# Two interleaved transformer layers on one core: a slot between producer and consumer at the seams, and layer norm's centring folded into the expert weights

## The chip, the cores and the metric

One core of one Trainium2 chip runs the whole model. The time is the device time of the core in microseconds (us), and the median of the runs counts. The core has TensorE (PE in the profile, its weight loads PEld), VectorE (DVE), ScalarE (ACT), GpSimd (POOL) and SyncE (SP, which issues all DMAs). Every engine works through its own stream of instructions in order, and semaphores tie the streams together.

## The reference, cut to what matters

The input is 4 sequences of 1024 tokens with 128 features. Four blocks follow one another, each with a residual and a layer norm:

```
x = layernorm(x + mamba(x))          # conv of 4 taps, 256 channels x 16 states, scan over time
x = layernorm(x + moe16(x))          # 16 experts of 64, top 2, and a shared one of 352, SiLU
x = layernorm(x + lstm_attention(x)) # LSTM of 20 cells over time, gives place and width of a Gaussian
x = layernorm(x + 4 x moe4(x))       # 4 layers of 4 experts of 512, top 2, GELU
```

Each of the four layers of the last block (layer 1's FFN) computes

```
logits = x @ router_w + rb;  comb = top-2 softmax weights
xhat = (x - mean(x)) * rsqrt(var(x) + 1e-5)
y_e = gelu((xhat * g_e + b_e) @ w1_e + b1_e) @ w2_e + b2_e
x = sum_e comb_e * (x + y_e)
```

All of it is in float32.

## The kernel before, in words

Time is cut into 8 chunks of 128 tokens (512 columns over the 4 sequences). The LSTM needs 1024 steps one after another; a step goes PE (gates, L905), ACT (L915, L916), DVE (L929, L932, L935), ACT (L919), DVE (L940). All other work is laid between these steps by hand. `period(i)` lays out 128 **slots**. In slot t each engine's stream gets the LSTM step t of chunk i, and then, in this order, one piece (up to a generator's next `yield`) of `layer1(i-1)`, `layer0(i+1)`, and of the Mamba work for chunk i+2 (`scan`, `leave`) and i+3 (`pre`, `soft`). A piece is what stands between two `yield`s, and the same piece number falls in the same slot on all engines. So where producer and consumer are in the same piece number, the consumer's engine waits inside the slot; where they are one piece apart, the result is usually there already.

- `layer1` of chunk q: attention for `att_slots(q)` = 18+q slots, then 4 layers of `LAYER` = 23 slots, then a last norm of 5 slots. In a layer, slots o = 0 to 4 are the norm and the router, o = 5 to 22 the experts (v = 0 to 17): the first product of unit v, L656, GELU, L714, the second product of unit v-2, L666.
- The norm (`norm_pe`, `norm_act`, `norm_dve`, `norm_pool`, L338 to L389): the mean by a product with a matrix of 1/128 (L337, in the layers two products, L623 and L625), centring (L372), square (L362), variance (L347), +EPS (L376), power -0.5 on POOL (L388), its rows by a product (L354), scaling (L381).
- The router (`choose_dve`, L395 to L428), the transposed weights `combT` (L644, L706), the load of the GELU table (L707) and of the exp table (L717, after the last GELU, o = 20).
- `layer0`: the 16-expert FFN in 11 units, each of three pieces: gate product (L465), up product (L469), down product (L475) on PE, tanh (L515) on ACT, three products by element on DVE (L556, L561, L546). It runs in the slots that are not `heavy` (o = 6 to 21 are heavy), from slot 4 on.
- `scan`: 64 pieces for 32 states, one in each heavy slot (L1197, L1206 on DVE, L1135, L1139, L1154 on POOL). `burst`: the decays (L1226, ACT), 8 per layer, in slots o = 22, 0, 1, 2, 3, behind all else in the slot.
- `pre`: conv of chunk i+3 (taps L955, SiLU L1007 and L1011, L983, L988, L995), after the last layer's slots.
- Period 0 has no layer 1; `fold` runs there: for each of the 16 experts of the four layers, b @ w1 (L1284) and w1 times g (L1299), stored to DRAM.
- Before period 0 the opening does chunks 0 and 1 of Mamba (`unit`) and layer 0 of chunk 0; period 8 has only layer 1 of chunk 7, without the LSTM.

The order in a slot, from `period`:

```
next(lstm, None)
if layer1: next(layer1, None)
heavy = layer1 is not None and slot >= att and 6 <= o < LAYER - 1 and slot < tail
if layer0 and not (heavy and slot < CH) and slot >= (L0_AT if layer1 else 0):
    next(layer0, None)
...
    elif heavy: advance(scan, "scan", SCAN)
    if layer1 and att - 1 <= slot < tail - 2:
        for _ in range({22: 1, 0: 2, 1: 2, 2: 2, 3: 1}.get(o, 0)): next(burst, None)
```

## Time and profile before

| | |
|---|---|
| median of 3 runs | 3133.24 us (3132.89 to 3133.72) |
| profiled execution, its own time | 3143.73 us |
| its span, first to last instruction | 3141.7 us |
| busy: PE / DVE / ACT / POOL | 81% / 62% / 44% / 34% of the span |
| granted TensorE clock, mean | 0.803 of 2.4 GHz |

The rows further down are of the profiled execution. No engine is busy all the time; the LSTM step ties them together, and a slot lasts as long as its slowest way round.

### The profile page before, as it was taken

What the parts mean: (1) busy time and instruction counts of PE and PEld (TensorE: products, weight loads), DVE (VectorE), ACT (ScalarE), POOL (GpSimd) and SP (SyncE); (2) the same over time, 40 slices, a digit from 0 to 9 for tenths busy, and PEclk for the clock granted to TensorE, in tenths of its full rate; (3) what the DMA queues carried; (4) which work ended last, traced back from release to release, by engine and by line L of the source; (5) the groups of instructions that cost most, each with busy time, mean ns of one, the idle gap of its engine ahead of it and who ended that gap; (6) DMA issues with size and microseconds to landing.
All of it is one profiled execution on the core that took longest, in us unless ns stands there. A gap on an engine that the chain in (4) does not pass through costs nothing.

```text
span 3141.7 us, 30770 instructions
## 1 busy us (share of the span) xinstructions
PE 2537.0 (81%) x7208; PEld 1271.2 (40%) x7208; DVE 1943.4 (62%) x6569; ACT 1386.7 (44%) x4620; POOL 1062.8 (34%) x913
## 2 busy tenths in 40 slices
PE   4776884479996989789886998788978997889598
PEld 1122443244444444344444443444444444444344
DVE  4857587357775777567766677577766555444422
ACT  3232433435544555445544554445534444444233
POOL 4735257104542445235432455244422001100200
PEclk7587655659996899878996899789978996788699
DMA  3231332003321233113220332122311220111021
GB/s 108 68 84 54 89 99 72 25 13 100 101 66 28 80 96 90 42 46 101 78 71 27 92 97 75 25 73 84 92 33 46 65 64 21 34 64 58 10 81 57
DMA packets 111774, 204.70 MB, mean 65 GB/s; under 512 B 14799, under 2 KB 24422, under 8 KB 111592
## 3 DMA queue, kind: packets, MB, share of 16 engines
q1 hardware_dynamic: 111592, 202.75, 22.1%
q8 instruction: 57, 0.93, 0.1%
q14 instruction: 125, 1.02, 0.1%
HBM read 195.36 MB, written 7.34 MB: 65 GB/s over the span
## 4 chain that ended last, share of the span: by engine, by line
PE 41%; DVE 28%; ACT 14%; issue 7%; POOL 1%; DVEq 0%; POOLq 0%; ACTq 0%
PE p_hid L656 8%; DVE state L1197 7%; PE p_turn L905 7%; PE p_misc L666 4%; ACT cell_t L919 4%; DVE cell L935 3%; DVE add_c L932 3%; PE p_acc L666 3%; DVE weighed L1206 2%; DVE p_turn L929 2%; PE p_misc L354 2%; PE p_gate L465 2%; DVE hist L940 2%; PE p_turn L475 1%; ACT cand L916 1%
## 5 line engine op out<-in xcount | busy, mean ns | idle before, releaser
L905 PEld LDWEIGHTS p_turn<-hist,w_hh 22*128 22x128 f32 x2048 | 371.6, 225 | 1148.2 <-DVE hist L940 1013.9
L905 PE MATMUL p_turn<-hist,w_hh 22*128 22x4 f32 x2048 | 457.3, 291 | 420.2 <-DVE hist L940 402.2
L656 PE MATMUL p_hid<-xhat,w 128*128 128x512 f32 x1024 | 581.8, 652 | 1.1 <-ACT hid L714 0.7
L919 ACT ACTIVATE cell_t<-cell 20x4 f32<-20x4 f32 x1024 | 207.7, 203 | 701.7 <-DVE cell L935 701.7
L1135 POOL TENSOR_TENSOR drive<-du,rows 128x512 f32<-128x512 f32 x256 | 473.4, 1849 | 63.2 <-DVE state L1197 44.9
L929 DVE SCALAR_TENSOR_TENSOR p_turn<-p_turn,cell 20x4 f32<-20x4 f32 x1024 | 170.7, 167 | 500.8 <-ACT p_turn L915 478.9
L714 ACT ACTIVATE hid<-p_hid,b1f 128x512 f32<-128x512 f32 x512 | 351.6, 687 | 243.1 <-PE p_misc L666 151.1
L388 POOL TENSOR_TENSOR n_rstd<-n_var,minus_half 128x4 f32<-128x4 f32 x56 | 62.0, 1108 | 1098.3 <-DVE n_var L376 1098.3
L1197 DVE TENSOR_TENSOR_SCAN state<-decay,drive 128x512 f32<-128x512 f32 x256 | 398.1, 1555 | 25.2 <-POOL drive L1139 15.7
L1154 POOL TENSOR_TENSOR y<-y,weighed 128x512 f32<-128x512 f32 x192 | 242.4, 1262 | 450.5 <-DVE weighed L1206 449.9
L940 DVE SCALAR_TENSOR_TENSOR hist<-p_turn,cell_t 20x4 f32<-20x4 f32 x1024 | 162.7, 159 | 275.6 <-ACT cell_t L919 275.6
L915 ACT ACTIVATE p_turn<-p_turn 96x4 f32<-96x4 f32 x1024 | 157.8, 154 | 349.1 <-PE p_turn L905 345.7
L666 PE MATMUL p_acc<-hid,w 128*128 128x512 f32 x512 | 275.3, 621 | 0.0
L666 PE MATMUL p_misc<-hid,w 128*128 128x512 f32 x512 | 264.1, 598 | 0.0
L1206 DVE TENSOR_TENSOR weighed<-state,rows 128x512 f32<-128x512 f32 x256 | 184.7, 722 | 7.9 <-DVE state L1197 0.5
L916 ACT ACTIVATE cand<-p_turn 32x4 f32<-32x4 f32 x1024 | 171.9, 168 | 25.2
L935 DVE SCALAR_TENSOR_TENSOR cell<-p_turn,add_c 20x4 f32<-20x4 f32 x1024 | 157.9, 154 | 35.3
L656 PEld LDWEIGHTS p_hid<-xhat,w 128*128 128x128 f32 x1024 | 160.3, 191 | 42.5 <-issue 26.5
L1169 PE MATMUL p_hid<-weighed,ident 128*128 128x512 f32 x128 | 113.7, 986 | 78.9 <-DVE weighed L1206 78.9
L1226 ACT ACTIVATE decay<-delta,a_neg 128x508 f32<-128x508 f32 x256 | 174.6, 710 | 2.2
L932 DVE SCALAR_TENSOR_TENSOR add_c<-p_turn,cand 20x4 f32<-20x4 f32 x1024 | 154.8, 151 | 31.6
L1139 POOL TENSOR_TENSOR drive<-drive,kc 128x4 f32<-128x4 f32 x256 | 143.2, 559 | 20.1
(204 smaller groups left out, 3161.5 us busy)
## 6 DMA issues: line engine op xcount, KB each, us to landing
rows<-rows_dram SPq DMA_DIRECT2D x128, 512.0 KB, 5.0
w<-w_dram SPq DMA_DIRECT2D x128, 256.0 KB, 2.7
w<-in_w2T SPq DMA_DIRECT2D x128, 256.0 KB, 2.7
comb_b<-comb_dram SPq DMA_DIRECT2D x64, 512.0 KB, 4.7
rows<-comb_dram SPq DMA_DIRECT2D x128, 128.0 KB, 2.9
w<-in_w1T SPq DMA_DIRECT2D x16, 256.0 KB, 2.8
w_dram<-w SPq DMA_DIRECT2D x16, 256.0 KB, 2.4
out_xT<-result SPq DMA_DIRECT2D x8, 256.0 KB, 2.5
```

Of the source, the lines that this page charges most:

```text
L656: nc.tensor.matmul(p_hid[:, v % 2, :], w1[:, v // FB, (v % FB) * P:(v % FB + 1) * P], xhat[:, :], start=True, stop=True).then_inc(g_h, 1)
L666: nc.tensor.matmul((p_misc1, p_acc1)[e % 2][:, :], w2[:, e, f, :], hid1[:, w % 2, :], start=(f == 0), stop=(f == FB - 1)).then_inc(g_y, 1)
L714: nc.scalar.activation(hid1[:, v % 2, :], p_hid[:, v % 2, :], ACT.Gelu, bias=b1f[:, l * UN + v:l * UN + v + 1]).then_inc(g_gelu, 1)
L905: nc.tensor.matmul(gate_bank(i)[:, :, t:t + 1], w_hh[:, :], before, start=False, stop=False, skip_group_check=True).then_inc(gates_done, 1)
L919: nc.scalar.activation(cell_t[64:64 + PE_, :], cell[32:32 + PE_, :], ACT.Tanh, scale=0.5).then_inc(cell_tanh, 1)
L929: nc.vector.scalar_tensor_tensor(out=gate(32), in0=gate(32), scalar=1.0, in1=cell[32:32 + PE_, :], op0=ALU.add, op1=ALU.mult).then_inc(kee ...
L932: nc.vector.scalar_tensor_tensor(out=add_c[32:32 + PE_, :], in0=gate(0), scalar=1.0, in1=cand[0:PE_, :], op0=ALU.add, op1=ALU.mult).then_i ...
L935: nc.vector.scalar_tensor_tensor(out=cell[32:32 + PE_, :], in0=gate(32), scalar=0.5, in1=add_c[32:32 + PE_, :], op0=ALU.mult, op1=ALU.add) ...
L1135: nc.gpsimd.tensor_tensor(flat(drive[:, n % 2, :, :]), du[:, j, :], rows[:, (u * S + s_) % ROWS, 0, :], ALU.mult).then_inc(driven, 1)
L1154: nc.gpsimd.tensor_tensor(y[:, j, :], y[:, j, :], weighed[:, n % 2, :], ALU.add).then_inc(y_summed, 1)
L1197: nc.vector.tensor_tensor_scan(flat(state[:, n % 2, :, :]), flat(decay[:, n % RING, :, :]), flat(drive[:, n % 2, :, :]), 0.0, ALU.mult, AL ...
L1206: nc.vector.tensor_tensor(weighed[:, n % 2, :], flat(state[:, n % 2, :, :]), rows[:, (u * S + s_) % ROWS, 1, :], ALU.mult).then_inc(weighe ...
```

## The change

- **Norm of the four expert layers.** The mean of w1 over its rows is taken off each expert's w1 once (in `fold`), so that `xhat` needs no centring: the square is taken of x itself, the mean comes as a fifth column of the router's product, and the variance is E[x2] + EPS - mean2. The two mean products (L623, L625) and the centring (L372) go for l = 0 to 3; the norm behind the last layer keeps them. New small DVE instructions: a copy of the mean, its square, and a subtraction in the place of the +EPS.
- **Norm slots.** Square in slot 0, variance products in 1, tanh in 2, `comb` in 3, rstd rows and xhat in 4. `combT`'s products move from slot 4 to v = 0, into another bank, its copy on ACT to v = 1 (o = 6), and its DMAs follow one slot later. The exp table is loaded one slot later (v = 16).
- **Fold.** Per expert one product of 128x512 more on PE and one subtraction of 128x512 on DVE, in the same piece.
- **Layer 0.** ACT's tanh and the DVE pieces behind it come one piece later; the down sum, the last norm and the copy get pieces between them (55 pieces for 52). It starts in slot 1 and leaves out slot o = 22.
- **Attention.** The third row product comes second, one DVE instruction of 128x512 less, the scans in two halves; one slot more (`att_slots` 19+q).
- **Conv (`pre`).** The second pair of taps comes a piece earlier, the SiLU of the second block, the second z product and its SiLU a piece later; one piece fewer in all.
- **Scan in the opening.** The product that sums `weighed` k on PE comes in the piece after the one that makes it.
- **Decays** come before layer 1 and layer 0 in ACT's stream.

```diff
@@ layer1_pe, per layer
-            ln = norm_pe(n1, q * NL + l, src, (n1.src_ready, q * NL + l + 1), logits, (lambda: mean_of_two(n)) if l else None)
-            for s_ in range(5):
-                next(ln)
-                if s_ == 4:
-                    pe.wait_ge(g_comb, n + 1)
-                    for j in range(B):
-                        mm = nc.tensor.transpose(p_hid[0:E1, 1, j * P:(j + 1) * P], comb1[:, j, :], ident[:, :])
-                    mm.then_inc(g_combT, 1)
+            pe.wait_ge(n1.src_ready, q * NL + l + 1)
+            for j in range(B):
+                mm = nc.tensor.matmul(p_hid[:, 0, j * (E1 + 1):(j + 1) * (E1 + 1)], tile(src, j), w_router1[:, l, :],
+                                      start=True, stop=True)
+            mm.then_inc(g_logit, 1)
+            yield
+            pe.wait_ge(n1.square_done, q * NL + l + 1)
...
+            for _ in range(3):
                 yield
+            pe.wait_ge(n1.rstd_done, q * NL + l + 1)
...
+                if v == 0:
+                    pe.wait_ge(g_comb, n + 1)
+                    for j in range(B):
+                        mm = nc.tensor.transpose(tile(p_acc1, j)[0:E1, :], comb1[:, j, :], ident[:, :])
+                    mm.then_inc(g_combT, 1)
@@ layer1_act, per layer
+            act.wait_ge(n1.src_ready, q * NL + l + 1)
+            if l:
+                act.wait_ge(n1.var_done, q * NL + l)
+            nc.scalar.activation(n1.square[:, :], src, ACT.Square).then_inc(n1.square_done, 1)
+            yield
+            yield
+            choose_act(n, arg1, tanh1, g_arg, g_tanh)
+            yield
+            yield
+            act.preload_act_table(ACT.Gelu)
+            yield
...
-                    if v == UN - 1 and l < L - 1 and q + 3 < NCH:
-                        act.preload_act_table(ACT.Exp)
+                if v == 1:
+                    act.wait_ge(g_combT, n + 1)
+                    if n:
+                        act.wait_ge(g_comb_stored, 16 * n)
+                    nc.scalar.copy(combT1[:, :], p_acc1[0:E1, :]).then_inc(g_combT_taken, 1)
+                if v == UN and l < L - 1 and q + 3 < NCH:
+                    act.preload_act_table(ACT.Exp)
@@ layer1_dve, per layer
+            yield
+            next(ch)
+            nc.vector.tensor_copy(mean1[:, :], p_hid[:, 0, 0:B * (E1 + 1)].rearrange("p (b e) -> p b e", b=B)[:, :, E1:E1 + 1]
+                                  .rearrange("p b o -> p (b o)")).then_inc(mean_step, 1)
+            next(ch)
+            dve.wait_ge(mean_step, 2 * n + 1)
+            nc.vector.tensor_tensor(mean1[:, :], mean1[:, :], mean1[:, :], ALU.mult).then_inc(mean_step, 1)
+            yield
+            dve.wait_ge(mean_step, 2 * n + 2)
+            dve.wait_ge(n1.var_done, q * NL + l + 1)
+            nc.vector.scalar_tensor_tensor(out=n1.var[:, :], in0=p_acc1[:, 448:448 + B], scalar=EPS, in1=mean1[:, :],
+                                           op0=ALU.add, op1=ALU.subtract).then_inc(n1.var_taken, 1)
+            next(ch)
+            yield
+            next(ch, None)
+            yield
+            dve.wait_ge(n1.rstd_rows, q * NL + l + 1)
+            nc.vector.tensor_tensor(xhat[:, :], src, p_misc1[:, :], ALU.mult).then_inc(n1.out_done, 1)
+            yield
@@ mamba_scan_pe
+            if early and k:
+                sum_y(k - 1)
             yield
-            if early:
-                pe.wait_ge(weighed_done, n + 1)
-                nc.tensor.matmul(p_hid[:, j, :], ident[:, :], weighed[:, n % 2, :], start=False, stop=(k >= NS - NB),
-                                 skip_group_check=True).then_inc(y_summed, 1)
             yield
@@ fold_pe
+            pe.wait_ge(fold_grown, k + 1)
+            if k:
+                pe.wait_ge(fold_scaled, k)
+            nc.tensor.matmul(p_misc1[:, :], mean_w[:, :], w1[:, k % E1, :], start=True, stop=True).then_inc(fold_mean, 1)
@@ fold_dve
+            yield
+            dve.wait_ge(fold_mean, k + 1)
+            nc.vector.tensor_tensor(w1[:, k % E1, :], w1[:, k % E1, :], p_misc1[:, :], ALU.subtract).then_inc(fold_scaled, 1)
@@ period
-    L0_AT = 4
+    L0_AT = 1
+    BURST = {LAYER - 1: 1, 0: 1, 1: 2, 2: 2, 3: 2}
...
+            if u < NCH and layer1 and att - 1 <= slot < tail - 2:
+                for _ in range(BURST.get(o, 0)):
+                    next(burst, None)
             if layer1:
                 next(layer1, None)
-            if layer0 and not (heavy and slot < CH) and slot >= (L0_AT if layer1 else 0):
+            last = layer1 is not None and att < slot < tail and o == LAYER - 1
+            if layer0 and not ((heavy or last) and slot < CH) and slot >= (L0_AT if layer1 else 0):
```

## Rows read from the trace of the kernel before

**Rows 1.** The page's head, and the granted TensorE clock in 40 slices:

```profile
span 3141.7 us, 30770 instructions
...
PEclk7587655659996899878996899789978996788699
```

**Rows 2.** Timeline of one bare LSTM step, period 2, slot 122 (start, us, what [idle before]):

```profile
1308.53 0.59 PE L905 MATMUL p_turn<-hist,w_hh 22*128 22x4 f32 x2 [1.57 <-DVE hist L940]
1309.15 0.15 ACT L915 ACTIVATE p_turn<-p_turn 96x4 f32<-96x4 f32 x1 [0.87 <-PE p_turn L905]
...
1309.33 0.17 DVE L929 SCALAR_TENSOR_TENSOR p_turn<-p_turn,cell 20x4 f32<-20x4 f32 x1 [0.86 <-ACT p_turn L915]
...
1310.12 1.28 ACT L1062 ACT_TABLE_LOAD   x1
1310.14 0.16 DVE L940 SCALAR_TENSOR_TENSOR hist<-p_turn,cell_t 20x4 f32<-20x4 f32 x1 [0.27 <-ACT cell_t L919]
```

**Rows 3.** Sums by stretch: the opening, period 0, period 3 (columns in the first row):

```profile
core 0: us, PE busy (x) PEld busy (x) DVE busy (x) ACT busy (x) POOL busy (x), PEclk, DMA share, GB/s
0.00:330.63 330.63, 210.69 (x352) 72.52 (x352) 212.57 (x228) 94.93 (x197) 171.91 (x161) 0.71 0.28 77
330.63:646.18 315.55, 193.68 (x536) 122.85 (x536) 202.03 (x671) 120.14 (x488) 132.19 (x114) 0.54 0.23 69
...
1319.42:1659.08 339.66, 293.22 (x856) 144.02 (x856) 234.35 (x816) 170.66 (x575) 138.92 (x117) 0.86 0.24 71
```

**Rows 4.** Seams of seven slots: worst, best, sums of 20 (periods 1-5), period 6, period 7:

```profile
1433.64:1458.88 25.24, 23.30 (x65) 11.64 (x63) 13.89 (x62) 13.18 (x37) 2.81 (x4) 0.71 0.21 59
...
2066.49:2085.04 18.55, 15.13 (x61) 7.91 (x60) 12.51 (x60) 14.21 (x39) 2.94 (x3) 1.00 0.19 60
...
sum 431.55, PE 387.38 PEld 199.26 DVE 271.06 ACT 270.22 POOL 57.73; mean PE 19.37 PEld 9.96 DVE 13.55 ACT 13.51 POOL 2.89
...
sum 75.08, PE 67.62 PEld 33.70 DVE 54.58 ACT 33.14 POOL 4.53; mean PE 16.91 PEld 8.43 DVE 13.65 ACT 8.29 POOL 1.13
...
sum 69.64, PE 55.27 PEld 37.73 DVE 36.01 ACT 28.77 POOL 4.03; mean PE 13.82 PEld 9.43 DVE 9.00 ACT 7.19 POOL 1.01
```

**Rows 5.** The same 20 stretches, the mean products of L623 and of L625 alone:

```profile
sum 431.55, PE 20.34 PEld 5.27; mean PE 1.02 PEld 0.26
...
sum 431.55, PE 15.35 PEld 6.32; mean PE 0.77 PEld 0.32
```

**Rows 6.** Single slots of period 3: o = 22, o = 1, and o = 19, 20 (columns as in rows 3):

```profile
1498.12:1501.99 3.87, 3.87 (x13) 1.54 (x12) 2.67 (x8) 1.90 (x6) 0.35 (x1) 0.85 0.42 157
...
1505.03:1507.90 2.87, 2.40 (x12) 1.48 (x12) 2.36 (x18) 2.38 (x7) 0.00 (x0) 1.00 0.00 0
...
1425.62:1428.00 2.38, 2.29 (x6) 0.97 (x6) 1.98 (x7) 1.11 (x4) 1.18 (x3) 1.00 0.64 195
1428.00:1431.32 3.32, 1.44 (x4) 0.59 (x4) 2.02 (x6) 2.59 (x6) 2.69 (x3) 0.95 0.19 72
```

**Rows 7.** Timeline of the worst seam's slot o = 0 (6.36 us long):

```profile
1439.05 0.69 DVE L372 TENSOR_TENSOR mdrive<-xl,p_misc 128x512 f32<-128x512 f32 x1 [1.68 <-PE p_misc L625]
...
1440.73 0.60 ACT L515 ACTIVATE silu<-p_gate 128x512 f32<-128x512 f32 x1 [3.55 <-PE p_gate L465]
...
1441.36 1.33 ACT L1226 ACTIVATE decay<-delta,a_neg 128x508 f32<-128x508 f32 x2
```

**Rows 8.** Who waited for whom over the whole run (us, times, longest):

```profile
PE p_hid L1169 <- DVE weighed L1206: 78.9, 60, 16.3
...
ACT xd L1007 <- PE p_hid L955: 28.5, 7, 8.6
...
ACT xd L1011 <- PE p_hid L955: 17.7, 8, 2.7
```

**Rows 9.** Period 0, 14 slots with fold and layer 0: stretch, and its costliest PE group:

```profile
383.40:427.63 44.23, 39.28 (x97) 21.27 (x96) 38.41 (x88) 14.99 (x61) 23.92 (x22) 0.57 0.43 134
...
L465 PE MATMUL p_gate<-mid_x,w_gate 128*128 128x512 f32 x10 | 9.4, 1042 | 0.0
```

**Rows 10.** The opening beside layer 0, 15 of chunk 1's 32 scans (columns as in rows 3):

```profile
191.50:251.10 59.60, 43.57 (x89) 16.06 (x87) 51.53 (x61) 19.23 (x45) 26.74 (x30) 0.97 0.35 96
```

**Rows 11.** Period 8, from the last expert's sum to the next layer's first product:

```profile
3016.44:3025.21 8.77, 6.70 (x33) 4.56 (x31) 4.90 (x26) 0.84 (x2) 1.01 (x1) 0.80 0.17 60
```

201 lines of the change are left out of this document (107 added, 94 removed).

## The prediction

> **What bounds the kernel now.** I read the page first, then one bare LSTM step, then sums by stretch, by seam and by slot, then the waits. The page has no full engine, and a granted TensorE clock that moves between tenths 5 and 9 [rows 1]. The bare step shows what a slot costs at least. From one L940 to the next it takes 1.83 us, and in it ACT is idle 0.87 us before L915 and DVE 0.86 us before L929 [rows 2]. So what else a slot gives to ACT or DVE is free up to about 0.9 us and then lengthens the slot one for one; PE has some 1.2 us (1.57 us idle, less its own turn-round). A period has 128 slots, 234 us if all were bare; period 3 takes 339.66 [rows 3]. The excess is in three places. The heavy slots (2.38 us for a plain one [rows 6]) hardly change. The **seams**, the seven slots o = 22, 0 to 5 between two expert layers, take 431.55 us for the 20 of periods 1 to 5, 21.58 each, and 18.8 and 17.4 in periods 6 and 7 [rows 4]. The rest is attention, the conv behind the last layer, and period 0.
>
> In a seam PE is busy 19.37 of 21.58 us, but 15.13 of 18.55 where the clock was 1.00, and 23.30 of 25.24 where it was 0.71 [rows 4]. So a seam has about 15.1 us of PE work at 2.4 GHz, and what makes the bad ones is that work at half clock with consumers waiting in the same slot. The worst slot says it: centring waited 1.68 us for the mean, layer 0's tanh 3.55 us for its gate product, and two decays of 1.33 us stood behind the tanh, ahead of the next LSTM step [rows 7].
>
> **The parts, costed.** The sum is made against the profiled execution, 3143.7 us, 10.5 above the median of the runs; I take the difference off the median.
>
> *Seams of periods 1 to 5.* The two mean products go: 1.02 + 0.77 = 1.79 us of PE a seam [rows 5], and with them the centring, 0.69 us of DVE [rows 7]. Slot 22 loses layer 0's piece. Slot by slot, with a 512-column ACT or DVE instruction at 0.6 to 0.75 us:
> - o = 22: DVE has 0.75 + 0.69; less 0.86 free gives 1.83 + 0.6 = 2.45. Before it was 3.87 in one case, with layer 0 in it [rows 6].
> - o = 0: ACT has a decay and the square, and in one seam slot of three layer 0's tanh: 2.3 or 2.8, mean 2.45.
> - o = 1: DVE has logits, four maxima, mean copy, mid, arg and the mean's square, 1.3 us, and layer 0's 0.69: 2.0 less 0.86 gives 2.95. Before: 2.87 [rows 6], bound by three ACT instructions.
> - o = 2: match-replace and var, 1.0, and layer 0: 2.7. o = 3: two decays, sometimes the tanh: 2.4. o = 4: the table of 1.28 us [rows 2], sometimes the tanh: 2.5. o = 5: PE has the LSTM, L656, the four transposes that moved here and layer 0: about 2.7 us of work, 2.5 after the slack of o = 4.
>
> That makes 18.0 at full clock. The seams' clock was not full (19.37 of PE time for 15.1 of work is a mean of about 0.8), and in a half-clock slot with variance products or rstd rows and a layer 0 product PE needs about 4.2 us and not 2.9. I add 1.0 for it: 19.0, so 2.6 less, times 20: **-52**.
>
> *Exp table* behind GELU 16 and not 15. Slot o = 20 takes 3.32 against 2.38 for the one before [rows 6]. In the next slot ACT has no GELU, and 1.28 less 0.87 stays under 2.38. 0.94 times 15 loads (three layers of periods 1 to 5): **-14**.
>
> *Conv and the end of layer 0.* The SiLUs waited for taps in their own slot, 28.5 + 17.7 us in all, in 7 and 8 waits of up to 8.6 us [rows 8]; the long ones must lie in the serial opening, where a step apart brings nothing. I take two waits of 1.3 us and 0.9 for layer 0's end, 3.5 for each of periods 1 to 4, and 1 for period 5, which has no conv: **-15**. Bounds 0 and -30.
>
> *Attention.* A DVE instruction of 0.69 goes, but four layer 0 pieces per period move here from slots 22, some 2 us of PE each at half clock (L465 1042 ns a matmul, two to a product, in a half-clock stretch [rows 9]). The one slot more here is one fewer bare slot behind the layers. I take **0**; bounds +25 and -25.
>
> *Periods 6 and 7* have no decays. Seams of 18.8 and 17.4 should come to 17.4 and 15.9 by the same table: **-11**. *Period 8* has no LSTM; from the last expert's sum to the next first product it takes 8.77 us [rows 11]. The chain loses the last mean product and the centring and gains the addition (about 1.1), and GELU no longer waits for a table behind the combT copy (about 0.5): three such seams and the first: **-6**.
>
> *Opening.* PE's products on `weighed` waited 78.9 us in their slot [rows 8], and layer 0's products stood behind them. Beside layer 0, 15 scans took 59.6 us with DVE busy 51.53 [rows 10]; the new order can save at most the difference, 8. I take -6, and -1 for each of three `pre`, whose second z product leaves the chain: **-9**.
>
> *Period 0* is where the change costs. 16 products of 128x512 and 16 DVE subtractions are added. In 14 slots there PE was busy 39.28 of 44.23 us and DVE 38.41, at clock 0.57 [rows 9]. The product costs about 2 us at that clock, the subtraction 0.7 us and a wait, as both are in one piece. If PE's free 11% takes half, 0.9 us is left per expert: **+14**. Bounds: 16 x 0.2 = +3, 16 x 2 = +32.
>
> Sum: -52 -14 -15 +0 -11 -6 -9 +14 = **-93**. 3143.7 gives 3050.7, and 3133.2 gives **3040**.
>
> The DMAs: the combine weights' store and the two loads (L1375, L1381) leave one to two slots later on SP; they are needed at o = 11, five heavy slots of 2.3 us on, so I give them nothing. Queued behind the SP wait are the rows of the scan, needed a slot later; I give that nothing either.
>
> **The rivals.**
>
> (a) *The clock falls in the seams, slower than before.* In period 7, without layer 0, PE has less to do in the seams, and a seam's PE time is 13.82 us of 17.4; in period 6 it is 16.91 of 18.8 [rows 4]; slices 31 to 33 of the clock, in period 6, read 899, and 34 to 38, over period 7, 67886 [rows 1]. The change takes 1.8 us of means and one layer 0 product out of the seams, so work of 15.1 becomes 12.5. If that lets the clock stay at 1.2 GHz through every seam, PE alone needs 25.0, against 21.58: +68 where I have -52, and +20 where I have -6 in period 6. Total 3143.7 + 53 and 3133.2 + 53 = 3186; with half of the seams' time so, about 3110. It decides against the kernel from a mean seam of about 23.6, a granted clock of 0.53 there. Against it: PE is busy 90% of a seam now and by my table 80% after, not less than in the heavy parts by much. Chance 0.04. [...]
>
> (b) *Most is eaten.* The seams stay tied by in-slot waits (21.0, -12), the conv gives 5, period 0 pays its upper bound +32, the rest as above: -12 -14 -5 -11 -6 -9 +32 = -25, or 3108. For it: period 0 has no free engine. Against: the worst slot names exactly the waits that go. Chance 0.11. This is also the case in which the steps between do not do what they say.
>
> (c) *More.* Seams of 18.0 (-72), conv -25, attention -15, period 0 +3 because the extra products lift its clock of 0.54: -149, or 2984. Chance 0.11.
>
> **How the numbers follow.** My forecast, -93, has 0.74; its own bounds (seams 18.4 to 20, period 0 +3 to +25, attention -15 to +15) give 3010 to 3075. The range goes to 3000 and 3100, between (c) and (b), and leaves out 2 in 10. A measurement of this kernel tells 0.2%, 6 us, from no change. Slower is (a), 0.04; within 0.2% the strip between (a) and (b), 0.03; faster 0.93.
>
> **What would show it.** Right: seams near 19 us, with slot 22 near 2.5; no L515 wait over 1 us beside layer 1; o = 20 near 2.4; period 0 longer by 3 to 30; the opening near 322 after 330.63 [rows 3]. Wrong: seams at 21 or more with a mean clock under 0.7; DVE's new subtraction waiting over 1 us for its product; GELU or the first weighting waiting for `comb_b`.

## The result, and the profile after

The changed kernel takes **3172.34 us** (median of 4 runs, 3171.75 to 3178.5); the kernel before, on the same chip, 3133.48 (3132.89 to 3136.19). The ratio is **1.0127**, 95% interval 1.0109 to 1.0144: 1.3% slower, where 3040 was forecast in a range of 3000 to 3100. The profiled execution after took 3171.77 us. The one before lay 10 us above its median, so the two spans differ by 28.3 us (3141.7 and 3170.0) and the medians by 38.9. The comparisons below are of spans.

The page's head, and the granted TensorE clock in 40 slices:

```profile
span 3170.0 us, 30665 instructions
...
PEclk6587675659985888769895889688978887678688
```

Against [rows 1] the row has more sixes to eights from its middle on (16 in the last 20 slices, where there were 11). The mean granted clock is 0.776, where it was 0.803.

Sums by stretch, columns as in [rows 3]: the opening, period 0, period 3:

```profile
0.00:321.56 321.56, 215.34 (x352) 68.78 (x352) 220.80 (x229) 96.35 (x197) 174.72 (x162) 0.72 0.28 79
321.56:649.88 328.32, 199.88 (x568) 119.60 (x568) 208.25 (x686) 121.52 (x488) 127.38 (x114) 0.61 0.22 66
1328.91:1669.20 340.29, 298.52 (x842) 146.52 (x842) 230.87 (x820) 170.85 (x575) 141.09 (x117) 0.83 0.24 71
```

The opening is 9 us shorter, period 0 is 13 longer, and period 3 gained nothing. Seams of seven slots, as in [rows 4]: a good one, the worst, the sum of the 20 of periods 1 to 5, period 6, period 7:

```profile
699.36:718.10 18.74, 17.18 (x59) 9.07 (x58) 11.86 (x61) 13.09 (x37) 2.45 (x3) 0.82 0.08 29
...
1853.85:1877.36 23.51, 22.15 (x58) 12.12 (x58) 12.64 (x62) 12.69 (x36) 2.81 (x4) 0.59 0.07 23
...
sum 429.07, PE 392.70 PEld 212.95 DVE 249.58 ACT 256.00 POOL 55.36; mean PE 19.64 PEld 10.65 DVE 12.48 ACT 12.80 POOL 2.77
...
sum 83.24, PE 75.45 PEld 41.69 DVE 49.29 ACT 30.66 POOL 4.03; mean PE 18.86 PEld 10.42 DVE 12.32 ACT 7.66 POOL 1.01
...
sum 68.72, PE 53.71 PEld 40.74 DVE 33.83 ACT 26.28 POOL 4.03; mean PE 13.43 PEld 10.19 DVE 8.46 ACT 6.57 POOL 1.01
```

Those 20 seams took 431.55 us and take 429.07. ACT has 14 us less to do in them and DVE 21 us less, but PE is busy 392.70 us, 5 more than before, although two mean products a seam are gone. The reader should look at the clock: it was 0.59 to 0.82 here, where [rows 4] had 0.71 in the worst seam and 1.00 in the best. Over all 20 the mean clock fell from 0.83 to 0.69. Period 6 went from 75.08 to 83.24.

One seam by slot, period 3 between the second and the third layer: o = 20, 21, 22, 0, 1 and 2. (A window runs from one L987 to the next, so the products of the code's slot 22 lie in the window of o = 21, the router's in that of o = 22, and so on.)

```profile
1503.05:1505.47 2.42, 1.44 (x4) 0.59 (x4) 2.02 (x5) 1.38 (x6) 2.42 (x2) 1.00 0.01 2
1505.47:1507.79 2.32, 1.44 (x4) 0.59 (x4) 1.92 (x6) 1.79 (x5) 1.62 (x3) 1.00 0.00 0
1507.79:1510.29 2.50, 1.32 (x7) 1.23 (x7) 2.07 (x6) 1.23 (x5) 0.34 (x1) 0.57 0.64 210
1510.29:1514.84 4.55, 4.55 (x15) 3.03 (x15) 1.32 (x6) 1.77 (x6) 0.00 (x0) 0.50 0.00 0
1514.84:1519.06 4.22, 4.22 (x9) 1.94 (x9) 2.22 (x15) 2.44 (x7) 0.00 (x0) 0.50 0.00 0
1519.06:1521.59 2.53, 2.28 (x4) 1.00 (x4) 2.09 (x17) 1.96 (x7) 2.25 (x2) 0.50 0.00 0
```

o = 20 and o = 22 are what the table said. o = 0 and o = 1 take 4.55 and 4.22 us at clock 0.50, and **PE is busy in all of it**. Of the 15 seams behind layers 0 to 2 of periods 1 to 5, 12 have the first length (4.54 or 4.55) and all have the second, at 0.50. The kernel before took 3.04 and 2.87 us in these two slots of the same seam; its o = 1 stands in [rows 6], and this is its o = 0:

```profile
1501.99:1505.03 3.04, 2.92 (x12) 1.31 (x11) 2.36 (x13) 1.85 (x6) 0.00 (x0) 1.00 0.16 59
```

Its clock was not full everywhere either. In the mean of those 15 seams it was 0.72, 0.80 and 0.99 in the windows of o = 21, 22 and 0, and it is 0.90, 0.68 and 0.50 after. So the half clock now lies over the slots in which PE has most to do. PE's timeline after, from the window of o = 22 to that of o = 1 (start, us):

```profile
1507.84 0.38 PE L952 MATMUL p_turn<-hist,w_hh 22*128 22x4 f32 x2 [0.89 <-DVE hist L987]
1509.35 1.87 PE L645 MATMUL p_hid<-w_router,xl 128*128 128x5 f32 x8 [1.13 <-DVE xl L876]
1511.08 2.05 PE L466 MATMUL p_gate<-mid_x,w_gate 128*128 128x512 f32 x2
1513.07 0.58 PE L952 MATMUL p_turn<-hist,w_hh 22*128 22x4 f32 x2
1513.58 1.87 PE L651 MATMUL p_acc<-mean_w,esig 128*128 128x1 f32 x8
1515.31 2.06 PE L470 MATMUL p_up<-mid_x,w_up 128*128 128x512 f32 x2
1517.29 0.58 PE L952 MATMUL p_turn<-hist,w_hh 22*128 22x4 f32 x2
```

From the router on PE never waits in the lines shown, and the LSTM's product (L952), whose sum the next slot hangs on, stands behind a router or variance of 1.87 us and a layer 0 product of 2.05.

Attention: the stretch from the first h of a period to the second last slot ahead of the first layer, sum over periods 1 to 5. Before, then after:

```profile
sum 253.45, PE 192.91 PEld 123.43 DVE 172.21 ACT 94.52 POOL 74.18; mean PE 38.58 PEld 24.69 DVE 34.44 ACT 18.90 POOL 14.84
```

```profile
sum 287.15, PE 240.04 PEld 139.82 DVE 184.80 ACT 99.86 POOL 77.78; mean PE 48.01 PEld 27.96 DVE 36.96 ACT 19.97 POOL 15.56
```

It holds one slot more than before, 1.83 us if bare, 9.2 for the five; the other 24.5 is growth. (The first h is the LSTM's first output of the period, the end of its first L940, or L987 after.) Part of one of its slots after, the one of period 4 that takes 5.1 us:

```profile
1678.37 2.08 PE L341 MATMUL p_gate<-xm,mean_w 128*128 128x512 f32 x2
...
1680.37 0.58 PE L952 MATMUL p_turn<-hist,w_hh 22*128 22x4 f32 x2
...
1680.99 0.15 ACT L962 ACTIVATE p_turn<-p_turn 96x4 f32<-96x4 f32 x1 [3.48 <-PE p_turn L952]
```

Layer 0's mean product (L341), here beside attention since L0_AT is 1, takes 2.08 us at half clock ahead of the LSTM's product, and ACT stands idle 3.48 us.

The waits of the run that the prediction named:

```profile
PE p_hid L1213 <- DVE weighed L1263: 60.6, 60, 12.8
...
ACT silu L520 <- PE p_gate L466: 28.9, 10, 4.1
...
ACT xd L1057 <- PE p_hid L1002: 24.6, 3, 10.8
...
DVE w L1363 <- PE p_misc L1349: 10.1, 8, 2.4
```

### The profile page after: what moved, and what is told of

Its sections match the earlier page's. It is cut to its first block, busy times and chain, and to the rows that moved or that the text cites. A ratio compares the mean times of both kernels' runs of the same rounds, so it can differ in the third digit from the quotient of the medians.

```text
span 3170.0 us, 30665 instructions
## 1 busy us (share of the span) xinstructions
PE 2616.6 (83%) x7128; PEld 1302.7 (41%) x7128; DVE 1939.3 (61%) x6610; ACT 1388.2 (44%) x4620; POOL 1067.9 (34%) x914
## 3 DMA queue, kind: packets, MB, share of 16 engines
q1 hardware_dynamic: 111976, 202.75, 21.5%
## 4 chain that ended last, share of the span: by engine, by line
PE 43%; DVE 30%; ACT 10%; issue 7%; POOL 1%; DVEq 0%; POOLq 0%; ACTq 0%
PE p_hid L668 9%; DVE state L1254 8%; PE p_turn L952 7%; PE p_misc L685 4%; ACT cell_t L966 4%; DVE cell L982 3%; DVE add_c L979 3%; DVE weighed L1263 3%; PE p_gate L466 3%; PE p_up L470 2%; PE p_turn L476 2%; PE p_acc L685 2%; DVE terms L863 2%; DVE p_turn L976 2%; PE p_misc L657 2%
## 5 line engine op out<-in xcount | busy, mean ns | idle before, releaser
L952 PEld LDWEIGHTS p_turn<-hist,w_hh 22*128 22x128 f32 x2048 | 379.0, 229 | 1097.4 <-DVE hist L987 875.8
L952 PE MATMUL p_turn<-hist,w_hh 22*128 22x4 f32 x2048 | 465.4, 295 | 315.0 <-DVE hist L987 297.9
L668 PE MATMUL p_hid<-xhat,w 128*128 128x512 f32 x1024 | 588.8, 658 | 6.8 <-DVE xhat L857 6.8
L966 ACT ACTIVATE cell_t<-cell 20x4 f32<-20x4 f32 x1024 | 207.7, 203 | 692.0 <-DVE cell L982 692.0
L987 DVE SCALAR_TENSOR_TENSOR hist<-p_turn,cell_t 20x4 f32<-20x4 f32 x1024 | 162.7, 159 | 275.5 <-ACT cell_t L966 275.5
L685 PE MATMUL p_acc<-hid,w 128*128 128x512 f32 x512 | 270.0, 611 | 0.0
L685 PE MATMUL p_misc<-hid,w 128*128 128x512 f32 x512 | 264.1, 598 | 0.0
L1263 DVE TENSOR_TENSOR weighed<-state,rows 128x512 f32<-128x512 f32 x256 | 192.2, 751 | 8.0 <-DVE state L1254 0.5
L1213 PE MATMUL p_hid<-weighed,ident 128*128 128x512 f32 x128 | 112.9, 980 | 60.6 <-DVE weighed L1263 60.6
## 6 DMA issues: line engine op xcount, KB each, us to landing
w<-w_dram SPq DMA_DIRECT2D x128, 256.0 KB, 2.7
w<-in_w2T SPq DMA_DIRECT2D x128, 256.0 KB, 2.7
w<-in_w1T SPq DMA_DIRECT2D x16, 256.0 KB, 2.7
w_dram<-w SPq DMA_DIRECT2D x16, 256.0 KB, 2.0
out_xT<-result SPq DMA_DIRECT2D x8, 256.0 KB, 2.6
```

The lines of the kernel that those rows point to most:

```text
L668: nc.tensor.matmul(p_hid[:, v % 2, :], w1[:, v // FB, (v % FB) * P:(v % FB + 1) * P], xhat[:, :], start=True, stop=True).then_inc(g_h, 1)
L685: nc.tensor.matmul((p_misc1, p_acc1)[e % 2][:, :], w2[:, e, f, :], hid1[:, w % 2, :], start=(f == 0), stop=(f == FB - 1)).then_inc(g_y, 1)
L952: nc.tensor.matmul(gate_bank(i)[:, :, t:t + 1], w_hh[:, :], before, start=False, stop=False, skip_group_check=True).then_inc(gates_done, 1)
L966: nc.scalar.activation(cell_t[64:64 + PE_, :], cell[32:32 + PE_, :], ACT.Tanh, scale=0.5).then_inc(cell_tanh, 1)
L1263: nc.vector.tensor_tensor(weighed[:, n % 2, :], flat(state[:, n % 2, :, :]), rows[:, (u * S + s_) % ROWS, 1, :], ALU.mult).then_inc(weighe ...
```

## Where the time went

Two traces cut into the same stretches, us (period 0 here up to the first h of period 1, and the opening up to the first h of period 0; the slot that moved to attention is taken off and added at 1.83 us, 12.8 for seven periods):

| stretch | before | after | difference | forecast |
|---|---|---|---|---|
| opening | 330.6 | 321.6 | -9.1 | -9 |
| period 0 | 317.4 | 330.2 | +12.8 | +14 |
| attention, periods 1 to 7, one bare slot less each after | 366.4 | 396.5 | +30.1 | 0 |
| seams, 1 to 5 | 431.6 | 429.1 | -2.5 | -52 |
| seams, 6 and 7 | 144.7 | 152.0 | +7.2 | -11 |
| heavy slots (o = 6 to 21), 1 to 5 | 773.0 | 761.8 | -11.2 | -14 |
| heavy slots, 6 and 7 | 286.2 | 288.6 | +2.4 | 0 |
| behind the layers, 1 to 7, one bare slot more each after | 284.8 | 282.6 | -2.2 | -15 |
| period 8 | 206.9 | 207.7 | +0.8 | -6 |

The rows give 28.3 in sum. Seams and attention hold 98 of the 121 us between -93 and +28.

How far one pair of traces can be trusted in a row shows from the runs below, which leave some stretches as they are. With the change's opening it took 319.1 to 326.0 us in twelve traces, with the old one 330.6, 326.2 and 327.8. Period 8 took 204.1 to 212.7 with the change and 205.3 to 210.1 without. So a row of some 5 us in these two is noise in part. Period 0 is firmer: 327.6 to 330.9 with the fold's products, 313.6 to 318.2 without.

## The experiments

Two theories stood against each other. The clock: in the slots ahead of the router PE has too little left to do, the clock falls to about half there (0.57 and then 0.50 in the windows above), and slots 0 and 1 are bound by PE's work at half clock. The moves: that layer 0's piece is missing from slot 22 and starts in slot 1 of attention costs by itself, whatever the clock. To tell them apart, an **unused product** (128x512, mean weights by a constant, into a PSUM bank that is free then; nothing reads it) fills a slot of PE without giving any other engine work (ACT and DVE are busy 255.5 and 249.6 us in the 20 seams of e12, which has 75 of them there, and 256.0 and 249.6 in the change's). Each run was compared with the kernel before on its own chip, and the ratios below are to that: its median was 3134.4 us beside e1 to e4, 3135.8 beside e5 to e8, 3145.0 beside e9 to e11 and 3136.1 beside e12 and e13. Microseconds of different groups can therefore be compared to some 10 us only; stretches are read from the traces.

```
+                nc.tensor.matmul(p_misc1[:, :], mean_w[:, :], w_in[:, :], start=True, stop=True)
```

### First four: fill, and undo one part each

**e1_fill**: the changed kernel, with the product behind L685 in the code's slots 21 and 22.

```
+                if v >= UN:
+                    pe.wait_ge(g_weighted, n * E1 + E1 - 1)
+                    nc.tensor.matmul(p_misc1[:, :], mean_w[:, :], w_in[:, :], start=True, stop=True)
```

> The changed kernel with one more product of 128x512 float32 on constants in slots o = 21 and o = 22 of every expert layer (into a bank that nothing reads before it is overwritten); nothing else is changed and no result uses it. Theory A (clock): in slots 21 and 22 PE now has only the LSTM step and one product, the clock falls to 1.2 GHz as slot 22 begins, and slots 0 and 1 then take 4.54 and 4.23 us in 18 of 24 seams with decays or layer 0. With the filler the clock should hold there: slots 0 and 1 near 2.5 and 2.9 us, the mean clock of the seams from 0.68 to over 0.85, less about 0.6 us a seam that the filler in slot 22 costs: 35 to 60 us faster than the changed kernel, below or near the kernel before. Theory B (order): slots 0 and 1 are long because the router's products wait for x on PE and layer 0's products queue behind them, whatever the clock; then the filler only adds PE work, and the kernel is 0 to 20 us slower than the changed one.

Measured: 3133.09 us (3125.91 to 3138.44), 0.9993 (0.9976 to 1.0011) of the kernel before: 39 us less than the change alone. The 20 seams of this kernel:

```profile
sum 402.70, PE 363.12 PEld 193.55 DVE 249.68 ACT 255.52 POOL 55.39; mean PE 18.16 PEld 9.68 DVE 12.48 ACT 12.78 POOL 2.77
```

That is 26 less than the change's. The products stand ahead of these windows, in those of o = 20 and 21, so the seams hold the same work, and PE is busy 363.12 us with it where it was 392.70. In the seams of period 3 behind layers 0 to 2, o = 0 takes 2.6 to 2.8 us and o = 1 still 3.9 to 4.2, at clock 0.50. The time is within theory A's 35 to 60, but the mean clock of the seams rose to 0.75 and not over 0.85.

**e2_slot22**: layer 0 in slot 22 again.

```
-            last = layer1 is not None and att < slot < tail and o == LAYER - 1
+            last = False
```

> The changed kernel with layer 0 allowed in slot o = 22 again. Theory A (clock): layer 0's product keeps PE busier in slot 22, so part of the falls at the seams go (the kernel before had a mean clock of 0.82 there): slot 22 longer by 0.7 to 1.4 us, slots 0 and 1 shorter by 3 us in about half of the seams, 5 to 30 us faster than the changed kernel. Theory B (order): only slot 22 gets longer, 15 to 25 us slower than the changed kernel. In both, attention gets no shorter, as layer 0 still starts in slot 1.

Measured: 3144.03 (3130.19 to 3147.95), 1.0022 (1.0005 to 1.0039). Seams 424.36; attention 282.18. The 28 us are theory A's in number, not in place: of the 27.5 us between the spans, the 20 seams give 4.7 and those of period 6 6.8, attention 5.0, the heavy slots 5 and the stretch behind the layers 4. In the seams o = 0 got 1.7 us shorter in the mean, but o = 1, which stays at clock 0.50, only 0.2, and o = 22 got 0.6 longer.

**e3_at4**: layer 0 starts in slot 4 again, and still leaves out slot 22.

```
-    L0_AT = 1
+    L0_AT = 4
```

> The changed kernel with layer 0 starting in slot 4, as before, and still not in slot 22. Theory C: the 30 us more that attention takes (beyond its one slot more) come from layer 0's first products beside the four row products of attention, on a PE at 1.2 GHz: slot 2 took 5.12 us against 3.12. Then attention gets 15 to 30 us shorter over the periods and the end of the periods a little longer: 10 to 25 us faster than the changed kernel. Rival: they come from the four pieces of layer 0 that moved into attention, wherever it starts; then starting later changes 5 us or less.

Measured: 3155.96 (3152.45 to 3160.38), 1.0065 (1.0044 to 1.0087), 16 less than the change. Attention of this kernel, periods 1 to 5:

```profile
sum 260.32, PE 200.64 PEld 124.56 DVE 172.27 ACT 97.55 POOL 73.89; mean PE 40.13 PEld 24.91 DVE 34.45 ACT 19.51 POOL 14.78
```

It is 27 less than the change's, about 1.8 us for each of the three pieces that left it in each of five periods, and within 7 of before, less than the 9.2 of its slots more. The rival is out. The pieces are done behind the layers instead, where the stretch grows by 11, and the seams grew by 7 (435.73).

**e4_both**: both edits undone, the rest of the change kept.

> The changed kernel with layer 0 placed as before: from slot 4 on and in slot 22 too. Theories A and C: the gains of both, 20 to 50 us faster than the changed kernel, that is between 15 us faster and 20 us slower than the kernel before. Theory B with the rival to C: 10 to 20 us slower than the changed kernel.

Measured: 3123.8 (3115.66 to 3132.69), 0.9964 (0.9948 to 0.998). The single edits gave -28 and -16, both together -48.5: they nearly add up. So the two moves of layer 0 cost 48 us, some 36 of them in attention by the traces, and without them the rest of the change is worth 10 us. The 20 seams are still as long as before:

```profile
sum 431.34, PE 398.57 PEld 212.58 DVE 258.58 ACT 259.07 POOL 55.25; mean PE 19.93 PEld 10.63 DVE 12.93 ACT 12.95 POOL 2.76
```

Layer 0 lies in them as before, and the two mean products are gone, so PE has less to do; yet it is busy 11 us longer than in [rows 4], at a mean clock of 0.68 where it was 0.83. This is the nearest that the runs come to the norm's change alone. No run puts the two mean products alone back. Both theories have their share: the moves are no small cost, and the seams that stay long at half clock are what is left.

### Next four: where a product pays, and the price of the fold

**e5_e4_21**: e4 with the product in slot 21 alone. **e6_e4_21_2_3**: also in slots 2 and 3 of each seam, where the layer's PE part has only an empty step:

```
-            for _ in range(3):
+            yield
+            for _ in range(2):
+                nc.tensor.matmul(p_misc1[:, :], mean_w[:, :], w_in[:, :], start=True, stop=True)
                 yield
```

> The changed kernel with layer 0 placed as before (slot 4 on, slot 22 too), and one unused product of 128x512 in slot o = 21 of every expert layer, where PE is busy some 1.3 of 2.3 us. Theory A (the clock falls because slots 21 and 22 leave PE idle): the seams' mean clock rises from 0.69 to over 0.78 and the seams get 2 to 3 us shorter each; 20 to 45 us faster than the run without the filler (3123.8), 3080 to 3105. Rival: layer 0's product in slot 22 already gives what the filler gave; then within 10 us of 3124.

> As the one with the filler in slot 21, and the same unused product in slots o = 2 and o = 3 of each layer too, where PE had 1.25 us of work in 2.4 to 2.9. Theory A: the clock is also held through the second half of the seam; 5 to 20 us faster than with the filler in slot 21 alone. Rival (PE work is what a seam lacks least): where the clock is at 1.2 GHz each filler lasts 2 us and delays the LSTM step; 10 to 30 us slower than with slot 21 alone.

Measured: e5 3121.21 (3116.48 to 3130.33), 0.9952 (0.9931 to 0.9972), within 3 us of e4, as its rival said: the seams' mean clock is 0.71, not over 0.78, and they are 0.5 us shorter each. e6 **3089.08** (3080.76 to 3095.07), 0.9833 (0.9796 to 0.9869), under both kernels, and 32 us under e5, where 5 to 20 were expected. The same seam as above in e6, o = 22, 0, 1, 2:

```profile
1479.29:1482.40 3.11, 1.95 (x12) 1.48 (x12) 2.68 (x8) 1.75 (x6) 0.35 (x1) 0.95 0.53 169
1482.40:1485.26 2.86, 2.86 (x10) 1.76 (x9) 1.32 (x5) 1.76 (x6) 0.00 (x0) 0.50 0.31 97
1485.26:1489.48 4.22, 4.22 (x9) 2.18 (x10) 2.22 (x15) 1.84 (x6) 0.00 (x0) 0.50 0.00 0
1489.48:1493.67 4.19, 4.19 (x8) 1.57 (x8) 2.09 (x17) 2.56 (x8) 2.59 (x3) 0.66 0.00 0
```

Against the change, the clock falls a slot later: o = 0 is mostly mended, o = 1 is not. That much e4 has already, by layer 0's piece in slot 22 (o = 0 2.8 us there in the mean). What the products in slots 2 and 3 do is seen behind o = 1: in the 15 seams behind layers 0 to 2, o = 2 got longer (3.7 us for 2.7 in e4), but o = 3 and o = 4 run at clock 1.00 where e4 has 0.51 and 0.77, and o = 4 takes 2.5 us for 3.6. The 20 seams come to 410.67.

**e7_before_21**: the old kernel with the product in slot 21, as e5.

> The kernel before with one unused product of 128x512 in slot o = 21. Theory A says that its bad seams, too, come from the clock: slots 20 and 21 there have the same PE work as in the changed kernel. The seams' mean clock rises from 0.82, and the kernel gets 5 to 30 us faster than before. Rival: before, the mean products and layer 0 in slot 22 held the clock, and the filler does nothing (within 5 us) or costs up to 10 us.

Measured: 3138.94 (3131.74 to 3149.38), 1.0003 (0.9986 to 1.0021): nothing in the whole. The 20 seams fell by 8 us (423.6), and the stretch behind the layers grew by 8.

**e8_nofold**: the changed kernel without the fold's 16 mean products and subtractions; the experts' weights stay uncentred, so this computes something else.

```
-            nc.tensor.matmul(p_misc1[:, :], mean_w[:, :], w1[:, k % E1, :], ...).then_inc(fold_mean, 1)
...
-            nc.vector.tensor_tensor(w1[:, k % E1, :], w1[:, k % E1, :], p_misc1[:, :], ALU.subtract)...
```

> The changed kernel without the centring of w1: the product with the matrix of means and the subtraction are left out in the fold, so that the expert layers compute with x times the power and not with centred x (their output is another one). It prices what period 0 pays. Theory: all 12.8 us that period 0 got longer are this product and this subtraction, and the rest of the kernel doesn't move: 10 to 14 us faster than the changed kernel (3158 to 3162). Rival: period 0 got longer by layer 0's three more pieces and the conv's other order; then 4 us or less.

Measured: 3156.75 (3150.69 to 3164.22), 1.0063 (1.0044 to 1.0082). Its first 50 slots of period 0, and then the same 50 of the changed kernel:

```profile
324.26:477.70 153.44, 127.54 (x334) 77.19 (x335) 118.01 (x321) 58.93 (x215) 68.62 (x64) 0.53 0.32 102
```

```profile
321.56:486.76 165.20, 133.37 (x366) 73.99 (x367) 122.59 (x337) 59.32 (x215) 65.55 (x64) 0.65 0.29 89
```

11.8 us for 16 experts, 0.74 each, so the theory holds for period 0. (The total lies 1 us under its range; other stretches than period 0 also differ between the two traces, by up to 6 us.) PE is busy only 5.8 us longer with 16 products more, as its clock is 0.65 there and not 0.53.

### Then three: is it the product or the change?

**e9_fold**: e6, with the subtraction one piece later than its product. **e10_free22**: e6, with slot 22 free of layer 0 as the change has it, and the product in slots 21, 22, 2 and 3. **e11_before_21_2_3**: the old kernel with the product in 21, 2 and 3.

> The kernel of e6 with the subtraction of the mean from w1 one piece later than the product that it subtracts, so that VectorE does not wait in the slot for TensorE. Theory (the fold's cost is in good part VectorE waiting for its product in the same piece): period 0 falls by 5 to 11 of the 12 us that e8 priced, and the rest stays as in e6: 3078 to 3085. Rival (the fold costs TensorE time at half clock, and the wait is only where it shows): period 0 falls by under 3 us, 3086 to 3092.

> The kernel of e6 with slot 22 without layer 0 again, as the change has it, and unused 128x512 products in slots 21, 22, 2 and 3. Theory (layer 0's absence from slot 22 cost only because the clock fell behind it): with the clock held, slot 22 stays at 2.5 us and not 3.3, slots 0 and 1 do not grow, and the seams are 1 us each shorter than in e6, less what the one slot more in attention gives back (1.8 us a period): 3070 to 3085. Rival (layer 0's work is TensorE work that has to be somewhere, and where it is makes no difference once the clock is held): 3089 plus up to 13 for the slots, 3089 to 3102.

> The kernel before with unused 128x512 products in slot 21 and in slots 2 and 3 of each seam. Theory (the old seams hold TensorE with two mean products already and their length is set by waits inside a slot, so products without a use gain little there): 3115 to 3140, and the change's steps between producer and consumer are what e6 gains over it. Rival (the products alone are worth the 35 us by which e6 is under e5, in whatever kernel they stand): 3090 to 3105, and then the change would be worth next to nothing even with the clock held.

Measured: e9 3093.27 (3083.88 to 3100.55), 0.9839 (0.9789 to 0.9889). The fold's 50 slots fell from 164.0 to 161.6 us and the rest of period 0 grew by 2.8, so period 0 as a whole fell by 0.4 and the rival holds: nothing to gain. e10 3096.82 (3088.49 to 3104.49), 0.9842 (0.9798 to 0.9886): slot 22 is 2.51 and not 3.11, but slot 1 still takes 4.1 in the mean at clock 0.50, so the seams are 408.5 and only 2 us shorter than e6's. What left slot 22 is done behind the layers, where the stretch takes 275.2 us for e6's 262.1. By ratio it equals e6 (0.9842 and 0.9833): the rival's 3089 to 3102, not the theory's 3070 to 3085. e11 3144.09 (3136.83 to 3147.15), 0.9991 (0.9973 to 1.001). Its seams:

```profile
sum 412.78, PE 371.22 PEld 191.43 DVE 270.31 ACT 270.03 POOL 57.89; mean PE 18.56 PEld 9.57 DVE 13.52 ACT 13.50 POOL 2.89
```

In periods 2 to 5 of e11 the mean clock of the seams was 0.92 to 0.96, and all 20 still take 20.6 us each in the mean; ten that had clock 1.00 throughout take 19.3. So the products did shorten the old seams, by 19 us, but something besides the clock holds them at 19.3, by [rows 7] probably the waits inside a slot. The whole gains nothing, as the seams of periods 6 and 7 grew by 11 us and attention and the stretch behind the layers by 6 each.

### Last two: does the table hold when the clock does?

Open was whether the 18.0 us of the forecast's table is there at all. Both kernels put the product into slots 0 and 1 as well, **e12_after_held** into the change as it stands (with 21, 22, 2 and 3 too), **e13_e6_0_1** into e6. The one in slot 0 is left out ahead of a period's first layer:

```
+            if l:
+                pe.wait_ge(g_weighted, n * E1)
+                nc.tensor.matmul(p_misc1[:, :], mean_w[:, :], w_in[:, :], start=True, stop=True)
             pe.wait_ge(n1.src_ready, q * NL + l + 1)
...
+            nc.tensor.matmul(p_misc1[:, :], mean_w[:, :], w_in[:, :], start=True, stop=True)
             pe.wait_ge(n1.square_done, q * NL + l + 1)
```

> The changed kernel as it is (layer 0 starts where the change has it, slot 22 without layer 0), with an unused 128x512 product in each of the slots 21, 22, 0 (ahead of the router's wait), 1 (ahead of the variance's wait), 2 and 3. Theory (the table of the forecast was right for full clock and only the clock was taken wrong): slots 0 and 1 take 2.3 to 2.6 and 2.9 us, the seams of periods 1 to 5 come to 17.5 to 18.5 each, mean clock over 0.9, and the whole to 3172 - 20 x 3.3 - 15 = 3085 to 3105, with attention still 30 to 40 us longer than before. Rival (the products' own time comes back, or the clock falls all the same on the many narrow products of router and variance): seams of 20 or more, slot 1 still over 4, 3115 to 3135 as with the two products of e1.

> The kernel of e6 with two more unused 128x512 products, ahead of the router's wait in slot 0 and ahead of the variance's wait in slot 1. Theory (what is left of the excess is the half clock in slot 1, and wide products there hold it): slot 1 falls from 4.2 to 2.9 us and slot 2 from 3.7 to 2.5, about 2 us in each of some 16 seams, clock there over 0.9: 3050 to 3065. Rival (narrow products of router and variance let the clock fall whatever stands before them): slot 1 stays over 4, and the total within 8 us of e6's, 3081 to 3097.

Measured: e12 3095.1 (3078.0 to 3095.61), 0.9845 (0.9811 to 0.988). e13 **3055.66** (3046.06 to 3058.72), 0.9733 (0.9709 to 0.9756), the fastest of all; both within their theory's range. (e12's seams are 18.9 us in the mean, not 17.5 to 18.5, for a reason told below; e13's o = 1 is 2.9 as expected, behind layers 0 to 2.) The same seam of period 3 in e12, o = 20 to 2 as above, and the sum of its 20 seams:

```profile
1475.70:1478.13 2.43, 2.29 (x6) 0.97 (x6) 2.03 (x6) 1.38 (x6) 2.43 (x2) 1.00 0.00 1
...
1480.45:1482.96 2.51, 2.08 (x13) 1.48 (x12) 2.08 (x6) 1.24 (x5) 0.34 (x1) 1.00 0.64 209
1482.96:1485.66 2.70, 2.70 (x13) 1.45 (x12) 1.32 (x5) 1.75 (x6) 0.00 (x0) 1.00 0.00 0
1485.66:1488.78 3.12, 3.12 (x13) 1.76 (x14) 2.22 (x16) 2.45 (x7) 0.00 (x0) 1.00 0.00 0
1488.78:1491.30 2.52, 2.52 (x8) 0.96 (x6) 2.08 (x16) 1.95 (x7) 2.25 (x2) 1.00 0.00 0
```

```profile
1480.45:1498.33 17.88, 17.21 (x67) 8.96 (x66) 12.71 (x61) 12.69 (x36) 2.81 (x4) 1.00 0.09 29
...
sum 377.27, PE 356.89 PEld 184.34 DVE 249.62 ACT 255.48 POOL 55.40; mean PE 17.84 PEld 9.22 DVE 12.48 ACT 12.77 POOL 2.77
```

This seam has four products more than the change's and takes 17.88 us where that took 22.51. PE's timeline in it has the unused product (L645), and then the same router (L648) and gate product as above, each in half the time:

```profile
1481.29 1.12 PE L645 MATMUL p_misc<-w_in,mean_w 128*128 128x512 f32 x2 [0.40 <-DVE terms L872]
1482.25 0.95 PE L648 MATMUL p_hid<-w_router,xl 128*128 128x5 f32 x8
1483.06 1.10 PE L466 MATMUL p_gate<-mid_x,w_gate 128*128 128x512 f32 x2
1484.10 0.38 PE L961 MATMUL p_turn<-hist,w_hh 22*128 22x4 f32 x2
```

And the seams and the clock of e13:

```profile
PEclk7587675658997799969996999779978997699699
```

```profile
sum 382.37, PE 361.28 PEld 187.21 DVE 258.50 ACT 258.18 POOL 55.22; mean PE 18.06 PEld 9.36 DVE 12.92 ACT 12.91 POOL 2.76
```

Fifteen of e12's 20 seams take 17.7 to 18.4 us, two 19.0, and three 22.1 to 22.5: these three follow attention, whose clock is 0.5 to 0.6. There o = 1 takes 5.93 us at half clock, 1.7 more than a half-clock o = 1 of the change (4.22), and these three seams took 19.6 to 19.9 us in the change. That is the price of the products where they fail to hold the clock.

## Why the prediction was wrong, point by point

**The step that failed is the clock's term in the seams.** It took the seams' clock from the kernel before, a mean of 0.8, and paid for it with 1.0 us a seam ("I add 1.0 for it: 19.0"), less than one slot at half clock by its own 4.2 for 2.9. But the clock is not given: it moved with the work that the change takes off PE. Layer 0's piece of slot 22 stood in the window of o = 21, which now has 1.44 us of PE as that of o = 20 has, and the mean products stood in the next one, ahead of the router. The clock fell from 0.83 to 0.69 over the seams. Slots 0 and 1 cost 4.55 + 4.22 = 8.8 us where the table had 2.45 + 2.95 = 5.4, so 3.4 a seam and not 1.0. The seams came to 429.1, not 380. That PE's work ahead of the seam matters is shown by e1, which adds two products ahead of the seam and shortens it (402.7 us for 429.1, at a mean clock of 0.75 for 0.69), and by e12 (377.3 us at 0.95). Which of the pieces taken away brought the fall is not separated: e2 gives layer 0's piece back and the mean clock stays at 0.68. The **table itself was right for full clock**: 15 of e12's seams have it and take 18.2 us in the mean for 18.0, with four products more in each, and single slots are 2.51, 2.70, 3.12 and 2.52 for 2.45, 2.45, 2.95 and 2.7. That e12's 20 seams come to 377.3, near the forecast 380, is in part luck, since three of them are at half clock in part and the forecast had 1.0 a seam for that.

This is **rival (a)'s mechanism**, which had 0.04. Its size was too large, since it put all seven slots at half clock (25.0 us) where two to five are (21.5); its total of 3186 lies near the 3172 by luck: its seams of periods 1 to 5 were forecast 70 us too long (+68 for -2.5), and attention (+30) and the conv (13 short), which it left alone, paid a good part of that. (By its own 25.0 for 18.8 period 6 would have been +25 and not +20.) Its mark of a mean seam of 23.6 for a slower kernel was not reached, 21.45 was enough, for the same reason. The weight was too small because the argument against it compared PE's busy share of whole seams, 90% before and 80% after. The rows that count here are those of the slots just ahead: what PE has to do in each, and at which clock the next one runs. In the change PE has 1.44 and 1.60 us to do in the windows of o = 20 and 21 (means of the 15 seams), and that of o = 22 runs at 0.68; in e1 it has 2.29 and 2.27, and that of o = 22 runs at 1.00. The two periods that the rival names were read and set aside: before the change the clock was 0.95 in the seams of period 6, with 16.91 us of PE in each, and 0.66 in those of period 7, with 13.82. (Of the rival's slices 34 to 38 the first lies mostly in period 6 and the last partly in period 8; over the whole periods the clock was 0.88 and 0.78.) In the seam shown above the clock falls behind the two windows with 1.44 us of work, and e12, which fills them, keeps 1.00. In the next two slots PE was busy 8.77 of 8.77 us and the clock stayed at 0.50. (The traces give the clock as a share of full speed. No run shows the 1.2 and 2.4 GHz of the forecast and the expectations; what the runs show in their place is 0.50 and 1.00, at which the same gate product takes 2.05 and 1.10 us.)

**Attention** was taken as 0 between bounds of 25 and failed: +30.1 over seven periods, beyond the upper bound, 24.5 of it in periods 1 to 5. The text had named the cause, four layer 0 pieces of some 2 us of PE at half clock, and then let them cancel against one DVE instruction. e3 shows it: with layer 0 back at slot 4 the five stretches fall by 26.8 us. PE is busy there 240 us of 287 after and 193 of 253 before, at a clock of about 0.56, so PE was not free for more pieces there.

**Conv and the end of layer 0**: -15 forecast, -2.2 measured (the stretch got 15.0 shorter, but 12.8 of that is the slot that went to attention). L1011's waits of 17.7 us in 8 [rows 8] are 8.2 in 3 (L1062), and L1007's 28.5 in 7 are 24.6 in 3. So 13 us of waits went and 2 us of time: either they were mostly not on the path, or layer 0's three more pieces took it back. No run tells which.

**Seams of periods 6 and 7**: -11 forecast, +7.2. It is the same failure in period 6 (+8.2, clock 0.95 before and 0.69 after); period 7 came 0.9 shorter where 6 was forecast, at 0.53 for 0.66. With products, e12 has 70.29 in period 6 and e13 61.69 in period 7.

**Right in kind and size**: the opening (-9.1 for -9, 321.56 for 322; that it fits to the tenth is luck, as the means of all traces of the two openings differ by 6, and PE's waits on `weighed` fell from 78.9 to 60.6 us); the exp table (o = 20 2.42 for 2.4, and heavy slots -11.2 for -14); slot 22 (2.50 for 2.45); period 0 (+12.8 for +14), which e8 prices at 11.8 for the fold. DVE's subtraction waited 10.1 us in 8 waits, the longest 2.4, so over 1 us in some, but it did not set the sum, as e9 says. The tanh's waits in the seams did go: of L515's there, 3.55 us in [rows 7], none is left (L520: its 28.9 us are ten waits in the opening). That was the change's aim, and it was reached, but the slot was then PE's. **Period 8**: -6 forecast, +0.8, and no difference in the mean of all traces with and without the change; what the shorter chain should have brought did not show, and why stays open.

The mark set for a wrong forecast, "seams at 21 or more with a mean clock under 0.7", did show: 21.45 us in the mean, at 0.59 to 0.82, and just under 0.69 over all 20.

**What the change is worth.** With the clock mostly held in the seams (0.93 to 0.95 in the mean): the old kernel's seams cost 412.8 (e11), the changed one's 382.4 (e13, layer 0 placed as in the old one) and 377.3 (e12). The pair is not quite even, as e12 and e13 have products in slots 0 and 1 too, and the old kernel was not run with those. Where the clock was 1.00 throughout, ten seams of e11 take 19.3 us in the mean and sixteen of e13 18.2: some 24 us for 20 seams is my estimate of what the steps between producer and consumer bring, and it shows only where the clock is held: e4's seams, at 0.68, take 431.3 us and the old kernel's 431.6. With products in slots 21, 2 and 3 alone in both, the seams are alike (410.7 in e6, 412.8 in e11); that e6 is 42 us shorter than e11 in the whole comes from the stretch behind the layers (29, of which 13 is the slot moved), the seams of periods 6 and 7 (13) and the heavy slots (11), against 12 more in period 0. The best kernel keeps the steps, moves layer 0 back to slot 4 and into slot 22, and fills five slots.

**Open**: why the first seam of a period is at half clock in part in three or four of five in e12 and e13 and not in the others (it has no product in slot 0 and no expert slots ahead of it to fill); an old kernel with products in slots 0 and 1; the mean products alone put back; and period 8.

## What to carry to other kernels

Before taking work off a busy TensorE, look at the granted clock of the slots that follow, and price the dense ones at half clock too, slot by slot, and not by a mean over the stretch: here slots 0 and 1, behind the lightened ones, ran at 0.50 and took 8.6 us in the mean behind layers 0 to 2, for 5.8 in e12 at 1.00, with two products more. Then try the change with an unused product in each slot that lost its work: where it held the clock here, fifteen seams of e12 took 18.2 us in the mean for the change's 21.5, and it may stay in the kernel; where it did not, it cost 1.7 us of a slot (5.93 for 4.22). Compare the length of the stretch and its clock, not the total alone. One slot filled was not enough to judge by here (e5 gained nothing over e4, e13 68 us). Where both a schedule's moves and its steps are changed, undo each alone: here the moves cost 48 us and hid the 10 us that the rest brought.
